# Routing the last block of tokens inside the experts' program: an attention and mixture-of-experts kernel on one Trainium2 core

## What is computed

```python
x = layernorm(x + attention(x) @ Wp.T)
probs = softmax(x @ Wg); topv, topi = top_k(probs, 2); gates = topv / sum(topv)
pos = (cumulative count of the expert among the choices before) ; keep = pos < cap    # cap = 1076
dest = where(keep, expert * cap + pos, dropped)
buf[dest] = x (each token twice); h = gelu(buf @ W1 + b1); y = h @ W2 + b2              # 8 experts, hidden 1024
out = layernorm(x + sum over the two choices of y[dest] * gate * keep)
```

## Time and profile before

| | |
|---|---|
| median of 3 runs (lowest, highest) | 1309.49 us (1307.85, 1310.57) |
| profiled execution | 1312.34 us, of it span of the instructions 1310.6 us |
| busy: PE, PEld, DVE, ACT, POOL | 1175.8, 506.3, 633.1, 919.3, 355.0 us |
| mean granted TensorE clock | 0.957 of full speed |

### The profile page before, as it was taken

The page is one execution under the profiler, slowest core; times in us unless marked ns, Lnnn a source line. Parts: engine busy times, 40 slices in busy tenths (PEclk is TensorE's granted clock), DMA queues, the critical chain, the costliest instruction groups (busy, mean ns, idle before and its releaser), DMA issues. The chain is left out here.

```text
span 1310.6 us, 24472 instructions
## 1 busy us (share of the span) xinstructions
PE 1175.8 (90%) x8759; PEld 506.3 (39%) x8759; DVE 633.1 (48%) x1751; ACT 919.3 (70%) x1203; POOL 355.0 (27%) x382
## 2 busy tenths in 40 slices
PE   7799999999999999998999899309999999999990
PEld 4222222222222222222222111106787787787780
DVE  5534342231374535625253201436777667667746
ACT  2688999999999999998999898115344345345314
POOL 2421211111130403224031300142533543543430
PEclk9999999999999999998999999559999999999995
DMA  6941231323330322222120100624415513421216
GB/s 154 186 111 56 81 85 56 79 65 91 74 108 19 112 38 91 60 68 65 60 87 4 39 3 8 200 81 127 112 18 125 124 23 107 116 23 20 27 21 256
DMA packets 83746, 104.24 MB, mean 80 GB/s; under 512 B 14937, under 2 KB 68932, under 8 KB 83632
## 3 DMA queue, kind: packets, MB, share of 16 engines
q1 hardware_dynamic: 66512, 77.74, 20.9%
q0 software_dynamic: 15744, 23.83, 8.7%
q10 hardware_dynamic: 1376, 1.18, 0.7%
HBM read 56.99 MB, written 48.29 MB: 80 GB/s over the span
## 5 line engine op out<-in xcount | busy, mean ns | idle before, releaser
L1354 ACT ACTIVATE prob<-ps_s 128x1024 f32<-128x1024 f32 (+3 forms) x854 | 719.6, 970 | 61.2 <-PE ps_s L1255 59.9
L1272 PE MATMUL ps_o<-prob,v_aug 128*17 128x512 f32 (+3 forms) x3294 | 444.1, 572 | 3.4 <-DVE acc L1416 1.5
L1255 PE MATMUL ps_s<-qop,kop 51*128 51x512 f16 (+3 forms) x1647 | 265.4, 370 | 22.7 <-ACT prob L1354 9.9
L1255 PEld LDWEIGHTS ps_s<-qop,kop 51*128 51x128 f16 x1647 | 61.9, 93 | 395.8 <-ACT prob L1354 372.7
L2100 PE MATMUL ps_y<-w2s,hs 128*128 128x256 bf16 (+1 forms) x1728 | 199.5, 273 | 1.8 <-DVE yb L2177 1.8
L1380 POOL TENSOR_SCALAR_AFFINE_SELECT prob<-prob 128x256 f32<-128x256 f32 (+1 forms) x180 | 70.8, 404 | 443.8 <-ACT prob L1354 441.1
L2147 ACT ACTIVATE hid<-ps_h,b 128x384 f32<-128x384 f32 (+1 forms) x192 | 105.1, 560 | 119.7 <-PE ps_h L2084 95.6
L2084 PE MATMUL ps_h<-xs,w1s 128*128 128x384 bf16 (+1 forms) x1152 | 182.2, 318 | 5.0 <-ACT hid L2147 4.2
L2100 PEld LDWEIGHTS ps_y<-w2s,hs 128*128 128x128 bf16 (+1 forms) x1728 | 167.3, 99 | 19.8 <-DVE yb L2177 2.3
L2041 POOL DMA_INDIRECT result<-y,entry x72 | 111.9, 1554 | 180.4 <-DVE y L2182 149.3
L1416 DVE COPY acc<-ps_o 32x512 f32<-32x512 f32 (+2 forms) x105 | 72.1, 687 | 182.3 <-PE ps_o L1272 180.5
(11 more groups left out here) (160 smaller groups left out, 712.1 us busy)
## 6 DMA issues: line engine op xcount, KB each, us to landing
w<-in_W SPq DMA_DIRECT2D x16, 1024.0 KB, 7.6
slots_x<-empty POOLq DMA_DIRECT2D x12, 520.0 KB, 3.9
qop<-fparts_q SPq DMA_DIRECT2D x42, 128.0 KB, 4.7
xe<-slots_x SPq DMA_DIRECT2D x8, 650.0 KB
x_all<-in_xT SPq DMA_DIRECT2D x8, 512.0 KB, 4.8
attnT<-acc SPq DMA_DIRECT2D x128, 32.0 KB
aT<-attnT SPq DMA_DIRECT2D x16, 256.0 KB
x_all<-in_x SPq DMA_DIRECT2D x8, 512.0 KB
```

The source lines that it names most:

```text
L1255: mm = pe.matmul(ps_s[:, u.p % SLOTS_S, e, a.q0:], o.key(e, a.h, a.kt), o.query(e, a.h, a.b, a.q0), start=True, stop=True)
L1272: mm = pe.matmul(ps_o[32 * c:32 * c + VW, a.q0:], o.v[:, a.kt, a.h], prob[:, t % RING, c % 2, c // 2, a.q0:], start=a.first, stop=a.last)
L1354: act.activation(prob[:, t % RING, n, e:z, q0:], ps_s[:, u.p % SLOTS_S, e:z, q0:], ACT.Exp, scale=1.0 / (SCALE * SCALE)).then_inc(exp_done, 1)
```

## The change

The last block is routed at the beginning of the experts' program, by a class `Last`; `route_last` and its meeting of all engines are gone.

- Loading: in attention, x of the last block is loaded at FLAG_TURN, and the sums and outputs of heads 8 to 15 at EARLY_TURN = 401, behind a wait for their stores. Only heads 0 to 7 are loaded behind the last store.
- DVE scales the two halves of `aT` apart, the early one first, and TensorE accumulates them in four banks. The statistics of a tile are taken right behind its add.
- The choice works on logits that aren't multiplied by the inverse root, and its steps are issued in turn with the root's. Normalizing (L1709 before) is done by ACT, tile by tile, with the high parts; the low parts by DVE, also those of the first expert's weights.
- POOL scatters a tile as soon as its own low part is there. SP waits for the scatters itself before it loads the experts' rows.
- TensorE issues WARM = 14 matmuls of 128x128 by 128x512 in f32 behind the count, into a bank that isn't read.

The diff, cut:

```diff
-LOAD_AT[BLOCK_END[NB - 1]] = NB - 1
+EARLY_TURN = max(j.end + LAG for j in JOBS if any(b == NB - 1 and h >= H // 2 for _, b, h in j.heads)) + 1
+assert FLAG_TURN < EARLY_TURN < N_TURNS - 8
+def stores_until(end):
+    return [max([j.stores for j in JOBS if j.number % ACCS == k and j.end <= end], default=0) for k in range(ACCS)]
...
+                        r.load_last_x(sp)
+                    if t == EARLY_TURN:
+                        for k, n in enumerate(stores_until(EARLY_TURN - LAG - 1)):
+                            sp.wait_ge(out_stored[k], n)
+                        r.load_last(sp, 1, f, r.early_loaded)
...
+    def load_last_x(r, sp):
+        n = NB - 1
+        sp.wait_ge(r.y_mm, (n - 1) * KT)
+        sp.wait_ge(r.split_low, n - 1)
+        sp.wait_ge(r.base_stored, 16 * (n - 1))
+        x = r.io["x"].rearrange("(n t p) d -> n p t d", t=KT, p=P)
+        sp.dma_start(r.x1[:, n % 2], x[n]).then_inc(r.last_loaded, 16)
+    def load_last(r, sp, c, f, signal):
+        n = NB - 1
+        cols = slice(n * QB, (n + 1) * QB)
+        sp.wait_ge(r.spread, n * KT)
+        sp.dma_start(r.total[0:P:DH, c], r.sums[bass.ds(f * H + c * (H // 2), H // 2), cols]).then_inc(signal, 16)
+        sp.dma_start(r.aT[:, n % 2, c], r.attnT[bass.ds(f * D + c * P, P), cols]).then_inc(signal, 16)
...
-def route_last(nc, io, psum, r, x):
-    n = NB - 1
...
-                x.load_weights(sp, io, 0, 0)
-                x.load_constants(sp, io)
-                x.load_weights(sp, io, 1, 1)
-                r.store_base(sp, n)
...
-                x.weights_low(pool, 0, 0, 0)
-                r.split_rest(pool, n)
-                for m in range(2 * KT):
-                    r.scatter(pool, n, m, r.scattered)
-                pool.wait_ge(r.scattered, NB * KT * 2 * 16)
...
+class Last:
...
+    def sync(l, sp, x, io):
+        r = l.r
+        f = sp.value_load(l.flag[0:1, 0:1], min_val=0, max_val=1)
+        for k, n in enumerate(stores_until(N_STEPS)):
+            sp.wait_ge(l.out_stored[k], n)
+        r.load_last(sp, 0, f, r.last_loaded)
+        x.load_weights(sp, io, 0, 0)
+        x.load_constants(sp, io)
+        x.load_weights(sp, io, 1, 1)
+        r.store_base(sp, l.N)
+        sp.wait_ge(r.scattered, NB * KT * 2 * 16)
+    def tensor(l, pe, out, count, warm):
+        r, u = l.r, l.N % 2
+        for c in (1, 0):
+            for s in range(KT):
+                pe.wait_ge(r.scaled, l.BASE + (1 - c) * KT + s + 1)
+                mm = pe.matmul(out[:, s, 0:D + E], r.aT[:, u, c, s * P:(s + 1) * P], r.wp[:, c, :], start=(c == 1), stop=(c == 0))
+                if c == 0:
+                    mm.then_inc(r.y_mm, 1)
+        r.pe_count(pe, l.N, count[:, 0:KT * E])
+        for _ in range(l.WARM):
+            pe.matmul(warm, r.aT[:, u, 0, 0:P], r.aT[:, u, 0, :], start=True, stop=True)
+    def scale(l, dve, c, s):
+        r, u, cols = l.r, l.N % 2, slice(s * P, (s + 1) * P)
+        step = (1 - c) * KT + s
+        if s == 0:
+            dve.wait_ge(r.early_loaded, 32)
+            if c == 0:
+                dve.wait_ge(r.last_loaded, 48)
+        if step >= 2:
+            dve.wait_ge(r.scaled, l.BASE + step - 1)
+        den = r.den[:, s % 2, c:c + 1]
+        dve.stream_shuffle(den, r.total[:, c:c + 1, cols], [0] * DH + [DH] * DH).then_inc(r.spread, 1)
+        dve.wait_ge(r.spread, l.BASE + step + 1)
+        dve.reciprocal(den, den).then_inc(r.inverted, 1)
+        dve.wait_ge(r.inverted, l.N + step + 1)
+        dve.tensor_tensor(r.aT[:, u, c:c + 1, cols], r.aT[:, u, c:c + 1, cols], den, ALU.mult).then_inc(r.scaled, 1)
...
+    def roots(l, dve):
+        r = l.r
+        c = Chain(dve, l.root, 0, RSQRT_STEPS + 1)
+        yield from rsqrt_pieces(c, r.mv[:, :, 1], [r.tmp[:, k] for k in range(5)], r.rstd[:])
+        c.wait()
+        c.did(dve.scalar_tensor_tensor(out=l.nmr[:], in0=r.mv[:, :, 0], scalar=-1.0, in1=r.rstd[:], op0=ALU.mult, op1=ALU.mult))
...
+    def choices(l, dve):
+        r = l.r
+        c = Chain(dve, l.choice, 0, 2 + 2 * KT + 4 + KT - 2)
+        l.chain = c
+        mean = r.mv[:, :, 0:1].broadcast_to([P, KT, E])
+        c.did(dve.tensor_tensor(r.shiftl[:], mean, r.wsum[:].unsqueeze(1).broadcast_to([P, KT, E]), ALU.mult))
+        yield
+        c.wait()
+        dve.wait_ge(r.logits_out, NB * KT)
+        c.did(dve.tensor_tensor(r.clogit[:], r.slogit[:], r.shiftl[:], ALU.subtract))
+        yield
+        c.wait()
+        for s in range(KT):
+            c.did(dve.max(r.top[:, s], r.clogit[:, s]))
+            yield
+        c.wait()
+        for s in range(KT):
+            c.did(dve.max_index(r.topi[:, s], r.top[:, s], r.clogit[:, s]))
...
+    def vector(l, dve, out, count, x):
+        r, n = l.r, l.N
+        for s in range(KT):
+            l.scale(dve, 1, s)
+        for s in range(KT):
+            l.scale(dve, 0, s)
+            if s >= 1:
+                r.dve_tile(dve, n, s - 1, out[:, s - 1])
+                l.stats(dve, s - 1)
+        r.dve_tile(dve, n, KT - 1, out[:, KT - 1])
+        l.stats(dve, KT - 1)
+        dve.wait_ge(l.stats_done, KT)
+        for s in range(KT):
+            dve.bn_aggr(r.mv[:, s], r.stats[:, s]).then_inc(l.stats_done, 1)
+        dve.wait_ge(l.stats_done, 2 * KT)
+        roots = l.roots(dve)
+        for _ in l.choices(dve):
+            next(roots, None)
+        for _ in roots:
+            pass
+        dve.tensor_tensor(l.drop[:], r.top[:, :, 1], r.top[:, :, 0], ALU.subtract).then_inc(l.applied, 1)
+        dve.wait_ge(l.applied, 1)
+        dve.tensor_tensor(r.gap[:, n % 2], l.drop[:], r.rstd[:], ALU.mult).then_inc(r.gap_done, 1)
+        dve.wait_ge(r.scattered, n * KT * 2 * 16)
+        dve.tensor_copy(r.xsplit[:, :, D:D + 1], r.number2[:, n].unsqueeze(2)).then_inc(r.tags, 1)
+        dve.tensor_copy(r.xsplit[:, :, D + 1:D + 2], r.chosen[:, :, 0:1]).then_inc(r.tags, 1)
+        c = Chain(dve, r.step, n * r.STEPS, 4)
+        r.place_rows(dve, c, n, count)
+        c.end()
+        r.weigh(dve, n)
+        for s in range(KT):
+            dve.wait_ge(r.split_high, n + s + 1)
+            dve.tensor_tensor(r.low[:, s], r.x1[:, n % 2, s], r.high[:, s], ALU.subtract).then_inc(r.split_low, 1)
+        for k in range(2):
+            x.weights_low(dve, 0, 0, k)
+    def scalar(l, act, x):
+        r, n = l.r, l.N
+        for k in range(2):
+            x.weights_high(act, 0, 0, 0, k)
+        act.wait_ge(l.root, RSQRT_STEPS + 1)
+        act.wait_ge(r.scattered, n * KT * 2 * 16)
+        for s in range(KT):
+            act.activation(r.x1[:, n % 2, s], r.x1[:, n % 2, s], ACT.Identity, scale=r.rstd[:, s:s + 1],
+                           bias=l.nmr[:, s:s + 1]).then_inc(r.x1_done, 1)
+            if s == 0:
                 r.act_gate(act, n)
-            @block.gpsimd
-            def _(pool):
-                x.weights_low(pool, 0, 0, 0)
-                r.split_rest(pool, n)
-                for m in range(2 * KT):
-                    r.scatter(pool, n, m, r.scattered)
-                pool.wait_ge(r.scattered, NB * KT * 2 * 16)
+            act.wait_ge(r.x1_done, n * KT + s + 1)
+            act.activation(r.high[:, s], r.x1[:, n % 2, s], ACT.Identity).then_inc(r.split_high, 1)
+    def gpsimd(l, pool):
+        r, n = l.r, l.N
+        for m in range(2 * KT):
+            if m == 0:
+                pool.wait_ge(r.dest_done, n + 1)
+                pool.wait_ge(r.tags, 2 * n + 2)
+                pool.wait_ge(r.gates, 2 * n + 2)
+            pool.wait_ge(r.split_low, n + m // 2 + 1)
+            alone(pool)
+            r.scatter_rows(pool, n, m, r.scattered)
...
+                last.sync(sp, X, io)
                 load(0, 0)
                 load(1, 1)
...
-                X.weights_low(pool, 0, 0, 1)
+                last.gpsimd(pool)
                 pool.wait_ge(r.base_stored, 16 * NB)
```

More of the change, by code:

```diff
@@ L1152, in attend @@
         evicted = sem("evicted")
-        out_stored = [sem(f"out_stored{k}") for k in range(ACCS)]
         empty_set = sem("empty_set")
@@ L1632, in spread_sums @@
         sp.wait_ge(r.inverse_stored, 16 * (n + 1))
-        r.load_total(sp, n, r.inverse)
+        for c in range(2):
+            sp.dma_start(r.total[0:P:DH, c], r.inverse[c * (H // 2):(c + 1) * (H // 2)]).then_inc(r.loaded[n % 2], 16)
     def pe_setup(r, pe, bank):
@@ L1768, in places, with place_rows @@
     def places(r, dve, n, bank):
-        c = r.chain
+        r.place_rows(dve, r.chain, n, bank)
+        r.chain.end()
+        r.weigh(dve, n)
+    def place_rows(r, dve, c, n, bank):
         dve.wait_ge(r.c_mm, n + 1)
@@ new lines, with __init__, stats @@
+class Last:
+    N = NB - 1
+    BASE = (NB - 1) * KT
+    WARM = 14
+    def __init__(l, r, flag, out_stored, sb, sem):
+        l.r, l.flag, l.out_stored = r, flag, out_stored
+        l.nmr = sb("last_nmr", [P, KT], F32)
+        l.drop = sb("last_drop", [P, KT], F32)
+        l.stats_done = sem("last_stats")
+        l.choice = sem("last_choice")
+        l.root = sem("last_root")
```

(46 more changed lines are left out.)

83 lines of the change are left out of this document (26 added, 57 removed).

## The result

The changed kernel takes 1298.44 us, the median of the three executions that can be compared (1298.14 to 1301.51; one that was disturbed is left out), against 1309.79 before: a ratio of 0.9916, 95% interval 0.9898 to 0.9934. It gained 11.4 us; 1289.2 us was predicted (20.3 won, range 1286.5 to 1296.5). The direction was right, the size missed by 9.2 us, and the time lies outside the range.

A forecast was written before the change was run, and what follows sets the result against it. The bound was a 60 us seam between attention and experts, one chain through other engines. 12.6 + 4.7 − 0.6 + 0.6 = 17.3, with 3.0 for the clock 20.3, off 1309.49: 1289.2 us, range 1286.5 to 1296.5.

The forecast's parts named there:

- Start of the seam: End of attention: early loads cost nothing, and DVE starts at 824.8 instead of 834.73, 0.5 us behind SP's last store.
- scaling in halves: DVE scales eight half units of 1.55 us instead of four of 2.6; statistics end at 841.4 instead of 854.0, 12.6 us less.
- The 3.8 us that I took for the collision: Part of the 12.6 us: a DVE product stood 4.20 instead of 0.42 us while POOL subtracted weights.
- Root and choice: DVE from aggregates to count: both chains alternate, 3.8 us (2.8 to 5.4) instead of 8.4; 4.7 us more won.
- Count to scatters: From DVE's count to POOL's first scatter: 3.6 us instead of 3.0, 0.6 lost; first scatter at 849.2.
- By the row it costs 0.1 us each and nothing in the sum: Price of DVE's subtractions beside POOL's scatters, from a scatter that took 1.06 in place of 0.98 us.
- the rival's size: Rival at the scatters: DVE's subtractions hold each scatter they meet for their whole length, 6.2 us, 1295.4 us; chance 0.11.
- Release: From the last scatter's end to the load of the experts' rows, 2.88 us before: 0.6 us won, bounds 0 and 1.65.
- Idle matmuls: TensorE behind the count: fourteen matmuls keep the clock at full speed for the experts' start, 3.0 us won (2.2 to 4.0).
- clock lost again: Rival: the pause between last idle matmul and rows is over 3 us and takes the 3.0 back, 1292.2 us; chance 0.13.
- the fast case: Idle matmuls with 4 us at half speed end at 861.9, leaving a pause of 2.9 us before the rows at 864.8.
- What is won in this chain moves the rest as a whole: Behind the seam: the experts simply follow sooner, since TensorE is 98% busy there; no cost was given.

The follow-up runs named there:

- before_pad56: The kernel before, with 56 semaphore instructions that do no work on TensorE at the end of the last routing: 1312.97 us against 1312.18 us (1.0018).
- root_first: loop20 with the interleaving undone, all steps of the root ahead of all steps of the choice: 1330.73 us on a slower chip, ratio 0.9875 to before.
- low_late: The changed kernel, with DVE's subtractions for the first expert's weights meant to wait until POOL has issued all scatters: 1298.49 us (0.9897).
- loop18_late: The changed kernel with 18 idle matmuls in a hardware loop, and DVE's weight subtractions waiting until all scatters have landed: 1295.17 us (0.9867).
- one_input: loop20 with DVE's two large two-input subtractions replaced by one-input products of the same size (output differs): 1325.49 us on a slower chip, ratio 0.9857.
- warm20: The changed kernel with 20 unrolled idle matmuls in place of 14: 1298.86 us (0.9899).
- loop20: The changed kernel with its 14 unrolled idle matmuls replaced by a hardware loop of 10 rounds of two (20 matmuls): 1296.01 us (0.9871).
- load_late: loop20 with early loading undone, both halves and x loaded behind the last store: 1334.55 us on a slower chip, ratio 0.992 to before.

## Why the prediction was right and wrong

- *Start of the seam, scaling in halves:* right. Counted from the last eviction the statistics end 18.46 us behind it; predicted were 841.4 − 822.95 = 18.45. The unit of 1.55 us is 1.54, and DVE's first instruction comes 0.53 us behind SP's last store (0.5 taken, and 0 for the boundary). The late half was issued 1.2 us later than taken, counted from the eviction, and kept nobody waiting. Of the 12.6 us, the early load makes 5.5; the rest is the use of halves as they land, with x off the way, and the end of the collision with POOL's subtraction. The 3.8 us that I took for the collision belong to the one execution read: in before_pad56 it cost 1.3. That the sum came out is due to its being set against that same execution.
- *Root and choice:* right. Predicted 3.8 us from the aggregates' end to the count, measured 3.5 (843.4 to 846.9). A step of the root cost some 0.06 us beside one of the choice (by the 1.8 us of root_first over 13 steps; 0.08 taken) and 0.20 alone.
- *Count to scatters:* right, 25.71 us behind the eviction against 26.25.
- *"By the row it costs 0.1 us each and nothing in the sum":* **this step failed**, by 2.5 us. I priced the port by one row in which an operation of 1.23 us lay beside a scatter of 1.06, and took its absence there for a rule. That scatter had begun 0.24 us ahead of the operation, so the row doesn't show the case that came. Here the second scatter took 2.52 and the third 1.90 us, and for each an operation had begun before it did. All 26 scatters that are stretched by the subtractions in the changed kernel and its variants (two in each of 13) end 0.84 to 0.86 us behind the end of such an operation: a scatter that meets a running one waits for the rest of it. Even the 0.08 us of the row fit that, for another operation ran ahead of the scatter and ended at 386.83, 0.85 us before the scatter did. The timeline of all engines in the kernel before:

```profile
386.13 0.70 DVE L689 CAST xs_half<-x_all 128x1024 f16<-128x1024 f32 x1
...
386.62 1.06 POOL L1830 DMA_INDIRECT slots_x<-xsplit,dest_all  x1 [0.31 <-issue]
386.86 1.23 DVE L692 TENSOR_TENSOR xs_half<-x_all,xs_half 128x1024 f16<-128x1024 f32 x1
```

  Neither is the rival's size, which took each scatter held for the operation's whole length and came to 6.2 in all: two scatters lost 1.54 and 0.92, and the small subtractions of 0.43 us cost nothing, for no scatter began within one. The rival's mechanism was the right one, and its price too high, since an operation holds only the scatter that meets it and only for what is left of it. In low_late the same two lengths moved with the operations, and in loop18_late they were gone. The Trainium skill, SBUF — State Buffer, Who interferes with whom, had it right: a Vector instruction with two SBUF inputs contends with a GpSimd one that reads SBUF. The same section lets a `tensor_scalar` contend as well where it runs in a two-port mode; one_input (1.21 to 1.37 us for 2048 columns, one scatter at 2.00) agrees with that, though its scatter ends 0.13 us behind the second operation and not 0.85. The section also infers that `tensor_tensor` leaves descriptor generation alone; these scatters were held all the same, and in which part of their work they were, no run shows.
- *Release:* right in kind, low in size: the load is issued 1.39 us behind the last scatter's end, so 1.5 won, not 0.6, inside its bounds (0 to 1.65). The rows' first transpose follows 3.12 us later (3.3 taken).
- *Idle matmuls:* **the price of the clock was right, and the step that failed is the length of the fourteen matmuls**, which cost 2.6 us of the 3.0. The first stage takes 9.6 us with the clock and 12.05 to 12.63 without it (2.4 to 3.0; 3.0 taken). But 14 matmuls took 14.0 us, not 15.9 to 17.7: the clock rose about 4 us after the first of them, the shorter of the two cases taken, and at full speed one took 0.89 us (six more took 5.3 in warm20), not 0.96. The stretched scatters put the rows later besides. So the pause was 6.1 us instead of 1.1 to 2.9, and the rival *clock lost again*, at 0.13, was the true case. Its chance was too low by the prediction's own rows: the sum of the fast case is off, since 2 matmuls in 4 us and 12 more at 0.96 us end at 861.6 and not 861.9, which makes the pause 3.2 us, over the 3 us after which the clock had fallen before. 20 matmuls mended it (warm20, loop20), but narrowly: root_first lost part of the clock after a pause only 0.3 us longer than loop20's.
- *Behind the seam:* **the step that failed most is one that isn't there.** I took what follows as moving as a whole ("What is won in this chain moves the rest as a whole"), and priced 56 new instructions on TensorE by their time alone. They shifted the expert loop's code, and its second round cost 4.0 us more in the profiled execution and 1.9 to 4.1 in the kernels above that have the stall. The trace of before could not give that price, but it had the fact: 1084 to 1180 us, in the loop's second round, has no instruction packet. The prediction's last line, expert stages longer than before, is how it showed.

The sum again, for the profiled span: 1290.3 predicted, plus 1.6 (eviction, within what executions differ by), 2.5 (scatters), 2.6 (clock), 4.0 (back edge), less 1.6 (release, rows and first scatter sooner than taken) is 1299.4.

## What to carry to other kernels

Unrolled filler on an engine that later runs a long hardware loop isn't free of code: compare the instruction queue's packets before and after, and write the filler as a loop. Keep large VectorE operations off indirect DMAs that lie on the path, whatever one harmless row says; look for the row where the operation is already running when the scatter begins. And idle matmuls are worth something only if they last nearly until the work arrives, so size them by the clock that they will themselves raise, with some to spare. A collision read in one execution can have another price in the next.

## What the runs showed of the hardware

- An expert loop whose place moves by 56 or 128 instructions is fetched again in its second round (77 packets instead of 67) and TensorE loses 1.9 to 4.1 us at the jump; with 28 or 256 it does not. The old kernel does the same with 56 (77 packets, 2.1 us).
- A scatter of 0.98 us that begins while an operation of 2.28 us with two SBUF inputs runs on VectorE ends 0.84 to 0.86 us behind that operation's end (26 of 26), so it takes 2.5 to 2.75 us or 1.90 by how much of the operation is left. One that begins first isn't stretched (0.99 us, the first scatter of the changed kernel). Beside two operations of 1.21 to 1.37 us with one input one scatter took 2.00.
- The other way round, VectorE's product of 0.42 us ends 0.3 us behind a running POOL subtraction of 4.06 us, and took 4.20 or 1.69.
- A semaphore increment behind indirect DMAs on POOL's queue ran with four scatters still to come.
- Granted full speed outlived pauses of 0.9, 1.3 and 1.4 us between idle matmuls and transposes (warm20, loop20, load_late). It was lost just before the first products after one of 1.1 us in loop18_late, and within them after one of 1.6 in root_first. The first products begin 3.2 to 3.6 us behind the idle matmuls in the three that kept it and 3.4 in loop18_late, so that doesn't tell them apart either; what does is open.
